# Layer 2 experts: index products spread between the up projection's products, and the start of the stage in another order

## The reference

```python
scores = jax.nn.softmax(xf @ gate_w.T, axis=-1)
topk_w, topk_idx = jax.lax.top_k(scores, K)             # K = 6 of E = 64
...
buf_tok = jnp.full((E, CAP), T, jnp.int32).at[sorted_e, pos].set(sorted_tok, mode='drop')   # CAP = 64
...
gx = xp[buf_tok]
gu = jnp.einsum('ech,ehi->eci', gx, gate_up_proj)       # H = 256, I = 96
g, u = jnp.split(gu, 2, axis=-1)
hid = jax.nn.silu(g) * u
eo = jnp.einsum('eci,eih->ech', hid, down_proj) * buf_w[..., None]
routed = jnp.zeros((T + 1, h), x.dtype).at[buf_tok.reshape(-1)].add(eo.reshape(-1, h))[:T]
shared = jax.nn.silu(xf @ shared_gate_w.T) * (xf @ shared_up_w.T) @ shared_down_w.T
```

## Time and profile before

| | us |
|---|---|
| median of 3 runs | 2366.07 (2353.83 to 2366.43) |
| the profiled execution's own time | 2379.67 |
| its span, first to last instruction | 2377.9 |
| first expert stage of layer 2, in the span | 909 to 1078 |
| second expert stage of layer 2, in the span | 1927 to 2101 |

### The profile page before, as it was taken

How to read it: one execution, slowest core, us unless ns; L and a number is a source line. 1 busy time by engine, 2 the same in 40 slices (tenths; PEclk the granted TensorE clock), 3 DMA queues, 4 the chain that set the end, 5 groups by cost and what they waited for, 6 DMA issues and landing times. The chain is left out here.

```text
span 2377.9 us, 52407 instructions
## 1 busy us (share of the span) xinstructions
PE 1959.3 (82%) x21293; PEld 1347.6 (57%) x21293; DVE 1212.3 (51%) x3208; ACT 835.6 (35%) x1973; POOL 469.8 (20%) x544
## 2 busy tenths in 40 slices
PE   7984779896999887656899999999998796559568
PEld 3542654565777554433666766766767655336445
DVE  6657541443564337624566666666665156252541
ACT  1012321221552222223576576676674022300120
POOL 0002410331000333631121221221220025500200
PEclk9997989896999998767899999999998887769679
DMA  4000000531500516741010010010000156450000
GB/s 156 0 6 9 1 5 1 161 143 37 213 1 7 176 48 192 254 160 48 20 39 21 21 39 21 21 39 20 21 21 3 36 157 211 137 165 3 10 6 19
DMA packets 55235, 157.39 MB, mean 66 GB/s; under 512 B 12803, under 2 KB 29785, under 8 KB 50726
## 3 DMA queue, kind: packets, MB, share of 16 engines
q1 hardware_dynamic: 43014, 126.74, 15.7%
q0 software_dynamic: 9888, 25.20, 3.3%
q10 hardware_dynamic: 2096, 2.10, 0.4%
HBM read 115.36 MB, written 40.48 MB: 66 GB/s over the span
## 5 line engine op out<-in xcount | busy, mean ns | idle before, releaser
L2165 PE MATMUL l_heads_ps_p<-xnT,l_heads_w 128*128 128x512 f32 x512 | 253.5, 620 | 8.3 <-DMA l_heads_w<-in_l_w_heads 8.3
L2565 DVE SCALAR_TENSOR_TENSOR l_heads_taps<-l_heads_padded,l_heads_conv,l_heads_taps 128x1024 f32<-128x1024 f32 x144 | 182.7, 1279 | 9.2 <-ACT l_heads_taps L2391 8.5
L2165 PEld LDWEIGHTS l_heads_ps_p<-xnT,l_heads_w 128*128 128x128 f32 x512 | 88.4, 191 | 79.9 <-issue 64.0
L206 PE MATMUL norm_turn<-zeros,ident 128*128 128x512 f32 x120 | 68.0, 724 | 57.1 <-PEq L60 57.1
L2740 POOL TENSOR_TENSOR l_heads_e<-l2a_table,l_heads_row 128x512 f32<-128x512 f32 x32 | 33.3, 1042 | 387.2 <-DVE l_heads_first L2576 382.3
L197 ACT ACT_TABLE_LOAD x10 | 12.8, 1283 | 245.3 <-PEq L60 245.3
L578 POOL TENSOR_TENSOR l_qkv_by_sin<-l_qkv_raw,l_qkv_angle 128x512 f32<-128x512 f32 (+1 forms) x16 | 23.2, 1451 | 314.3 <-ACT l_qkv_raw L566 310.9
L379 PE MATMUL l_ffn_a_ps_w<-l_ffn_a_term,ident 128*128 128x512 f32 x240 | 76.8, 473 | 8.6 <-DVE l_ffn_a_term L477 8.6
L206 PEld LDWEIGHTS norm_turn<-zeros,ident 128*128 128x128 f32 x120 | 27.0, 234 | 92.6 <-issue 92.6
L2391 ACT ACTIVATE l_heads_taps<-l_heads_ps_p,l_heads_conv 128x512 f32<-128x512 f32 x96 | 76.0, 792 | 0.0
L2390 ACT COPY l_heads_padded<-l_heads_ps_p 128x512 f32<-128x512 f32 x96 | 56.5, 589 | 50.9 <-PE l_heads_ps_p L2165 50.8
(11 more groups left out here) (694 smaller groups left out, 4898.6 us busy)
## 6 DMA issues: line engine op xcount, KB each, us to landing
l_results<-zeros SPq DMA_DIRECT2D x24, 512.0 KB, 6.3
l_ffn_a_w_in<-in_l_in_w SPq DMA_DIRECT2D x8, 1536.0 KB
l_ffn_b_w_in<-in_l_in_w SPq DMA_DIRECT2D x8, 1536.0 KB
l_heads_w<-in_l_w_heads SPq DMA_DIRECT2D x16, 512.0 KB
l_heads_row<-l_rows SPq DMA_DIRECT2D x16, 512.0 KB
l_ffn_a_w_out<-in_l_out_w SPq DMA_DIRECT2D x8, 768.0 KB
l_ffn_a_w_in<-l_results SPq DMA_DIRECT2D x8, 768.0 KB, 7.9
l_ffn_b_w_out<-in_l_out_w SPq DMA_DIRECT2D x8, 768.0 KB
```

The source lines that it names most:

```text
L206: pe.matmul(turn[:, i % KC, (i // KC) % HALVES, :], core.ident[:], core.zeros[:, 0:HALF], start=True, stop=True)
L2165: mm = pe.matmul(ps_p[half][:], w[b][:, which, c, :], core.xnT[:, c, half * HALF:(half + 1) * HALF], start=(c == 0), stop=(c == KC - 1))
L2565: dve.scalar_tensor_tensor(out=taps[which][:], in0=padded[which][:, :, j:j + SEQ], scalar=conv[p % 2][:, which, j:j + 1], in1=taps[which][ ...
```

## The change

Three places move. Nothing is added or taken away in the computation; the number of instructions is that of before apart from waits.

1. In the loop, `index(g + 2)` is no longer a block behind `up(g)`. Its eight rounds (one token tile, four small products) are issued one by one behind each of the eight products of `up(g)`'s second half. The waits of the index (`index_waits`: `found_ready` and `hot_ready`) stand ahead of that second half. The second `up_filled` is raised by the last product of `up`, which is behind seven of the eight rounds.
2. On DVE, `locate(1)` stands ahead of `add_shared(1)`, `one_hot(2, ...)` is split around it, `add_shared(3)` and the product `prob * chosen` go into group 0 of the loop. The order within PE follows: `turn_i(1)` and `turn_x(0)` ahead of `shared_out_of(2)`, and `shared_out_of(3)` between `turn_i(2)` and `turn_x(1)` in group 0.
3. On POOL, the third gather of group 0 goes ahead of the shared expert's third product.

```diff
@@ -1,3 +1,4 @@
+import itertools
 import math
 from contextlib import ExitStack

@@ -2963,9 +2964,9 @@
             shared(0)
             shared(1)
             pool.wait_ge(xn_stored, 16)
-            take(0, range(1))
+            take(0, range(PAIRS - 1))
             shared(2)
-            take(0, range(1, PAIRS))
+            take(0, range(PAIRS - 1, PAIRS))
             shared(3)
             take(1)
             pool.wait_ge(*cleared)
@@ -3008,17 +3009,23 @@
                                        parts[:, i, 2 * q:2 * q + 2, :].rearrange("p j i -> p (j i)"), start=(i == 0), stop=(i == TILES - 1))
                     mm.then_inc(i_filled, 1)

-            def index(g):
-
+            def index_waits(g):
                 pe.wait_ge(found_ready, count_of(g - 1))
                 pe.wait_ge(hot_ready, hot_count(g, PAIRS - 1))
+
+            def index_round(g, i):
+                for q in range(PAIRS):
+                    e = g * EG + 2 * q
+                    mm = pe.matmul(bank_l[ROWS * q:ROWS * q + 6, 0:P], parts[:, i, e:e + 2, :].rearrange("p j i -> p (j i)"),
+                                   hot[g % 2][:, q, i].rearrange("p j s -> p (j s)"),
+                                   start=(i == 0), stop=(i == TILES - 1), tile_position=(0, ROWS * q))
+                if i == TILES - 1:
+                    mm.then_inc(i_filled, 1)
+
+            def index(g):
+                index_waits(g)
                 for i in range(TILES):
-                    for q in range(PAIRS):
-                        e = g * EG + 2 * q
-                        mm = pe.matmul(bank_l[ROWS * q:ROWS * q + 6, 0:P], parts[:, i, e:e + 2, :].rearrange("p j i -> p (j i)"),
-                                       hot[g % 2][:, q, i].rearrange("p j s -> p (j s)"),
-                                       start=(i == 0), stop=(i == TILES - 1), tile_position=(0, ROWS * q))
-                mm.then_inc(i_filled, 1)
+                    index_round(g, i)

             def turn_i(g):
                 pe.wait_ge(i_copied, g)
@@ -3039,16 +3046,22 @@
                 b = g % 2
                 pe.wait_ge(w_loaded[g % SETS], 32 * (g // SETS + 1))
                 pe.wait_ge(x_read, KC * (g + 1))
+                rounds = iter(range(TILES if g + 2 < GROUPS else 0))
                 for q in range(PAIRS):
                     if q % 2 == 0 and g >= 1:
                         pe.wait_ge(hidden_ready, 2 * (g - 1) + q // 2 + 1)
+                    if q == PAIRS // 2 and g + 2 < GROUPS:
+                        index_waits(g + 2)
                     for c in range(KC):
                         for j in range(2):
                             e = 2 * q + j
                             mm = pe.matmul(up_of[q // 2][BOTH[j], q % 2, :], xgT[b][:, c, e * S:(e + 1) * S],
                                            w_in[g % SETS][:, e, c, :], start=(c == 0), stop=(c == KC - 1))
-                    if q % 2 == 1:
-                        mm.then_inc(up_filled, 1)
+                            if q % 2 == 1 and c == KC - 1 and j == 1:
+                                mm.then_inc(up_filled, 1)
+                            if q >= PAIRS // 2:
+                                for i in itertools.islice(rounds, 1):
+                                    index_round(g + 2, i)

             def turn_h(g):
                 if g >= 1:
@@ -3095,21 +3108,21 @@
             shared_out_of(0)
             shared_out_of(1)
             index(1)
-            shared_out_of(2)
             turn_i(1)
             pe.wait_ge(shared_taken, UNITS)
             turn_x(0)
-            shared_out_of(3)
-            pe.wait_ge(shared_added, TILES // 2)
+            shared_out_of(2)
             for g in range(GROUPS):
                 up(g)
-                if g + 2 < GROUPS:
-                    index(g + 2)
                 turn_h(g)
                 if g + 2 < GROUPS:
                     turn_i(g + 2)
+                if g == 0:
+                    shared_out_of(3)
                 if g + 1 < GROUPS:
                     turn_x(g + 1)
+                if g == 0:
+                    pe.wait_ge(shared_added, TILES // 2)
                 down(g)
             pe.wait_ge(diagonal_ready, len(BY_PE) * TOP2)
             for n, i in enumerate(BY_PE):
@@ -3271,15 +3284,13 @@
             for q in range(1, PAIRS):
                 one_hot(1, q)
             add_shared(0)
+            locate(1)
+            for q in range(PAIRS // 2):
+                one_hot(2, q)
             add_shared(1)
-            locate(1)
+            for q in range(PAIRS // 2, PAIRS):
+                one_hot(2, q)
             add_shared(2)
-            add_shared(3)
-            for q in range(PAIRS):
-                one_hot(2, q)
-            dve.wait_ge(exp_done, TILES)
-            step(dve.tensor_tensor(prob[:], prob[:], chosen[:], ALU.mult))
-            settled()
             for g in range(GROUPS):
                 for i in range(2):
                     dve.wait_ge(gate_ready, 2 * g + i + 1)
@@ -3289,9 +3300,15 @@
                                       up_of[i][:, :, F2:], ALU.mult).then_inc(hidden_ready, 1)
                 if g + 2 < GROUPS:
                     locate(g + 2)
+                if g == 0:
+                    add_shared(3)
                 if g + 3 < GROUPS:
                     for q in range(PAIRS):
                         one_hot(g + 3, q)
+                if g == 0:
+                    dve.wait_ge(exp_done, TILES)
+                    step(dve.tensor_tensor(prob[:], prob[:], chosen[:], ALU.mult))
+                    settled()
                 if g < TOP2:
                     weigh(g)
                 if g == TOP2 - 1:
```

## The result

The changed kernel takes 2374.52 us, median of 11 runs (2369.73 to 2381.22), against 2359.95 us (2353.13 to 2372.09, 11 runs) for the kernel before on the same chip. The ratio is 1.0066, 95% interval 1.0049 to 1.0083, or some 15.6 us slower. The forecast was +5.2 us: the sign is right and the time lies in the range, but the loss is three times the forecast's, near the rival "the switches are dear" (+18).

A forecast was written before the change was run, and what follows sets the result against it. No engine is full; a loop of dependences through PE's `up`, ACT and DVE sets each stage. Head -3.0 plus loop +8.2 gives +5.2 us on 2366.07, so 2371, range 2348 to 2388.

The forecast's parts named there:

- the switches are dear: Rival for `up`'s second half: each round shows its weight loads, 0.301 us; +18 us, 2384; chance 0.22.
- The price of a round: Index rounds in `up`'s second half: seven rounds lengthen it by 1.0 us, bounds 0.54 and 2.1.
- The upper bound: In `up`'s second half each round exposes loads of 0.086 and 0.137 us; seven rounds cost 2.1 us.
- The rule of the Trainium skill: For `up`'s second half: loads overlap matmuls only on different row groups, so switches would cost 2.1 us.
- The moved wait: Ahead of `up`'s second half PE waits for `hot` up to 1.8 us; quick groups with it lose 1.2 us.
- 2.5 to 5 groups: Expert loop: that many groups a stage pass on 1.1 us each, 2.8 to 5.5 us; middle 4.1.
- every second group: Expert loop: at best only every second group passes its loss on, as gathers follow `hidden`; 2.8 us a stage.
- The head: Start of both expert stages: `up(0)` and `up(1)` start earlier; -3.0 us for two stages, bounds 0 and -6.
- The signature: Start of the stage: `up(0)` starts 2.8 us behind the start of `turn_x(0)`, where it was 3.6.
- late completions shrink: Rival on PE in the expert loop: spreading the dense index removes late completions, 17.3 us, giving 2354; chance 0.20.
- The base: Whole kernel: forecast built on the profiled execution of 2379.67 us, its 13.6 us above the median carried along.

The follow-up runs named there:

- dummies alone: Kernel before plus one unread bf16 strip product behind each product of `up`'s second half; the half took 4.5 us, the kernel 2348.84 us in one execution.
- wait_only: Kernel before with only the index's two waits moved ahead of `up`'s second half, index still one block behind `up`; 2354.79 us, ratio 1.0001.
- second trace: Kernel before, unchanged, profiled once more; 2355.51 us in that execution.
- loop_only: Kernel before with the index spread through `up`'s second half, old order of the start kept; 2385.40 us, ratio 1.0125.
- head_only: Kernel before with only the new order of the start on PE, DVE and POOL, index one block behind `up`; 2352.41 us, ratio 0.9984.
- dummy_strip_timed: Kernel before plus one unread bf16 strip product behind each product of `up`'s second half, timed on a slower chip; 2398.12 us, ratio 1.0051.
- one_block: The changed kernel with all eight index rounds behind the first product of `up`'s second half; 2353.66 us, ratio 0.9980 against the kernel before.

## Why the prediction was right or wrong

**The price of a round: the step that failed.** The forecast had "1.0 us" for seven rounds, with bounds 0.54 and 2.1. Measured is 4.6 - 1.1 = 3.5 us (dummies alone 3.4), beyond the upper bound, and 4.8 to 5.7 at the lower clock. I was wrong "if a round costs ... over 0.25 us more than `up` alone"; it costs 0.45. The upper bound was built from exposed weight loads (0.086 and 0.137), one of each, though a round has four loads and a product of `up` two. The trace had the better hint: 326 ns is the length of one instruction, a product has two of them and still follows the last one after 173, so products overlap. Whatever parts them costs that overlap as well as its own time. A bound for a switch should have been the whole of one product and one small product with nothing overlapped. The two instructions of one product stand 0.163 us apart in the trace of before, so that is 0.163 + 0.326 + 0.219 - 0.173 = 0.54 us a round, or 3.7 us for seven, and the measured 0.45 and 3.5 lie inside it.

The rule of the Trainium skill that spoke against the change ("TensorE: Matmul & The Clock Gate", "Part 3: Packing small matmuls — row/col tiling") had the right sign but not the cause. By it any switch on the same rows shows the load; the runs show that on the same rows a 64-column bf16 product between 64-column products costs 0.03 us, one of another width some 0.45.

**The moved wait.** "A PE wait for `hot` of up to 1.8 us" is what the trace shows (1.80 and 1.91). By itself it cost nothing that can be measured (`wait_only`), presumably since it takes the place of later waits. The half starts behind it, though, and so the slow half has no cover on its own side.

**How much reaches the end.** I took 2.5 to 5 groups in each stage at full price. From the second trace of before to that of the changed kernel the two stages grew by 349.1 - 330.6 = 18.5 us; in `loop_only` by 33.3, or 2.8 us for each of 12 groups. The twelve halves of `loop_only` are together 71.4 us long instead of some 14, so they alone add 57.8 us, 4.8 a group, as most ran at the lower clock. So some 60% of that arrives, within the share of "2.5 to 5 groups", but by another way than "every second group": the waits for gathers are no fixed delays that shift, they shrink from 29.0 us to 4.1, and filled idle time gives clock back to `turn_x` and `down`. That these two make up the rest is argued from single traces and was not tested by itself.

**The head.** Forecast -3.0, measured -3.8 us by the ratio (interval -7 to -0.5). The signature was wrong: `up(0)` is 4.4 us behind `turn_x(0)`, not 2.8. The turn takes 1.89 us and the shared product 2.79 behind PE's wait, where they took 1.07 and 1.89. PE in `head_only`:

```profile
938.50 1.89 PE L3041 MATMUL l_ffn_a_bank_x<-ident,l_ffn_a_xg 128*128 128x128 f32 x8 [1.69 <-DMA l_ffn_a_xg<-l_xn_rows,l_ffn_a_take_at]
940.19 2.79 PE L2997 MATMUL l_ffn_a_bank_e<-l_ffn_a_shared_out,l_ffn_a_shared_hidden 96*128 96x256 f32 x8
942.90 2.82 PE L3055 MATMUL l_ffn_a_bank_u<-l_ffn_a_w_in,l_ffn_a_xgT 128*64 128x192 f32 x32
945.66 0.62 PE L3019 MATMUL l_ffn_a_bank_l<-l_ffn_a_hot,l_ffn_a_parts 128*6 128x128 bf16 x32
```

The gain is right behind it, where the index no longer waits 2.08 us for `one_hot(2)`: from `up(0)` to `up(1)` it is 8.5 us instead of 10.8. In the second stage that distance did not shrink (10.4, against 10.4 and 9.2 in the two traces of before), so this explains the first stage only. In the changed kernel's own trace `turn_x(0)` waited 6.24 us for its gather and `up(0)` started at 949.18, later than the 946.14 of before; where the head gains is thus not the same in every execution.

**The rival "late completions shrink".** It rested on one execution. The changed kernel has none in groups 0 to 6, and neither has the kernel before in its second trace. They came back in all four traces of the two chips where before takes 2384 us. In three of these the rows show that the index block itself is issued slowly, one to three products every 0.71 us, PE waiting for nothing that the profile shows. The same stands in the trace that the prediction was made from, and I overlooked it there: the index block behind `up` of group 1, just where the gates are late, is spread over 6.4 us in the first stage and 6.8 in the second, where in the second trace every index block starts all its products within 0.4. PE in the kernel before, first trace:

```profile
960.92 0.22 PE L3018 MATMUL l_ffn_a_bank_l<-l_ffn_a_hot,l_ffn_a_parts 128*6 128x128 bf16 x1 [0.48 <-issue]
961.63 0.27 PE L3018 MATMUL l_ffn_a_bank_l<-l_ffn_a_hot,l_ffn_a_parts 128*6 128x128 bf16 x4 [0.49 <-issue]
```

That execution took 2379.67 us, longer than any of the 11 timed runs of its kernel (up to 2372.09) and within what the slower chips show. PE in `dummy_strip_timed`:

```profile
964.35 0.22 PE L3018 MATMUL l_ffn_a_bank_l<-l_ffn_a_hot,l_ffn_a_parts 128*6 128x128 bf16 x1 [0.22 <-issue]
965.06 0.24 PE L3018 MATMUL l_ffn_a_bank_l<-l_ffn_a_hot,l_ffn_a_parts 128*6 128x128 bf16 x3 [0.49 <-issue]
965.79 0.22 PE L3018 MATMUL l_ffn_a_bank_l<-l_ffn_a_hot,l_ffn_a_parts 128*6 128x128 bf16 x1 [0.49 <-issue]
...
967.99 0.33 ACT L3154 ACTIVATE l_ffn_a_gate<-l_ffn_a_bank_u 128x192 f32<-128x192 f32 x1 [6.84 <-remote]
```

ACT's gate idles 6.84 us meanwhile. Why PE's instructions come slowly there, and whether it goes with the chip or with the execution, is open; no run was made for it. Whether the change would do better than before on such a chip is open too.

**The base.** The profiled execution was 13.6 us above the median, and I carried its rows (late gates, long waits) into groups that mostly don't have them. That the time lies in the range owes something to luck, by opposite errors: the price too low by a factor of 3.5, and most of the cover unseen.

The best kernel measured is the start of the change without the spread (`head_only`, 0.9984). An index whose products are 64 columns wide was not tried (the 0.03 us is for one such product behind each of `up`, not for the four of a round); `wait_only` and `one_block` suggest that there is little to win with it, as the block behind `up` is already hidden.

## What to carry to other kernels

On TensorE look at the distance of products, not only at their length: where it is shorter than the length, they overlap, and here a product of another column width between them took that away, 0.45 us each time. If small products must stand among large ones, put them in one lot (here 0.9980 to 1.0009 of before instead of 1.0066) or try to give them the same width. Before you price a delay, sum up the waits that it can fill (here 29 us for gathers), and see that it does not stand behind a wait of its own; and look at more than one execution before a stall of some microseconds becomes part of a forecast.

## What the hardware showed that I had not expected

- Price by column width: extra products of 64 columns between those of `up` cost 0.03 us each in bf16 (1.38 - 1.14 over 7) and 0.12 in fp32 (2.01 - 1.14 over 7), of 128 columns or in a 32-column strip 0.5 each (4.6 - 1.1 over 7), and an fp32 one in a strip 0.64 (5.65 - 1.14 over 7).
- No price shows for the change of PSUM bank: 1.3 us with 5 products in `up`'s own bank, 1.4 with 7 in another.
- Two pairs of chips differ by 28 us (2355 and 2357, 2384 and, from a single run, 2385) for the same kernel. Three of the four traces from the slower pair show PE's index block issued in pieces, and none of the eight from the other pair does. Of the two traces of the first comparison, that of before (2379.67 us) shows it and that of the change (2377.39 us) does not.
